# Two-stage kernel (log-space mixture, then attention over 32 images): the second stage's output taken in pieces of 1024 columns, and its fp32 products in two groups an image

## What is computed

```
x = x + L0(gn(x), accumulators)       # per position: log(exp(xs - max) @ exp(log_w - max)) + max + max
x = x + L1(gn(x), adj_w, affine_w, affine_b, ln_g, ln_b)

def L1(z):                            # z: 1024 x 128 for each image
    n = z / norm(z)                   # every row to length 1
    A = softmax(5 * (n @ adj_w @ n.T))            # 1024 x 1024
    h = A @ (z @ affine_w.T + affine_b)
    h = (h - mean(h)) / sqrt(var(h) + 1e-5) * ln_g + ln_b    # over the 128 channels
    return where(h >= 0, h, 0.01 * h)
```

## Time and profile before

| | |
|---|---|
| median of 3 runs | 1130.65 us (1130.39 to 1132.24) |
| the profiled execution | 1132.57 us, span 1130.8 us |
| busy share of the span | TensorE 93%, weight loads 70%, ScalarE 81%, VectorE 73%, GpSimd 49% |
| mean granted clock of TensorE | 0.988 |
| the chain that ended last | TensorE 85%, VectorE 7%, DMA 5% |
| HBM read, written | 136.45 MB, 20.31 MB |

### The profile page before, as it was taken

The page is one execution under the profiler, slowest core; times in us unless marked ns, Lnnn a source line. Parts: engine busy times, 40 slices in busy tenths (PEclk is TensorE's granted clock), DMA queues, the critical chain, the costliest instruction groups (busy, mean ns, idle before and its releaser), DMA issues.

```text
span 1130.8 us, 20986 instructions
## 1 busy us (share of the span) xinstructions
PE 1048.1 (93%) x7392; PEld 792.4 (70%) x7392; DVE 829.1 (73%) x1577; ACT 915.3 (81%) x1806; POOL 554.1 (49%) x391
## 2 busy tenths in 40 slices
PE   0189999959999999999999999999999999999995
PEld 0155555547777777777777777777777777777773
DVE  7822555588777777777777788787777777777776
ACT  0499999537888888888888888888888888888885
POOL 0044455503455555555555555555555555555543
PEclk9999999969999999999999999999999999999998
DMA  8979999830122222224322222222222222222213
GB/s 356 391 307 377 416 409 396 336 131 20 66 76 82 79 76 76 76 77 144 131 82 76 76 76 77 79 90 81 87 78 79 82 76 75 76 83 78 75 57 95
DMA packets 46903, 158.15 MB, mean 140 GB/s; under 512 B 5848, under 2 KB 6732, under 8 KB 36556
## 3 DMA queue, kind: packets, MB, share of 16 engines
q1 hardware_dynamic: 46796, 156.78, 37.2%
HBM read 136.45 MB, written 20.31 MB: 139 GB/s over the span
## 4 chain that ended last, share of the span: by engine, by line
PE 85%; DVE 7%; DMA 5%; ACT 1%; issue 1%; POOL 1%; SPq 0%; POOLq 0%; DVEq 0%; ACTq 0%
PE PS L1143 23%; PE PS L1144 21%; PE PS L1145 21%; DMA Wt<-acc 5%; PE PS L1161 5%; PE PS L1120 4%; DVE st L688 4%; PE PS L1110 3%; PE PS L1155 3%; PE PS L1131 2%; PE PS L1149 2%; DVE Pl L856 0%; PE PS L1178 0%; POOL hl L397 0%; ACT ET L457 0%
## 5 line engine op out<-in xcount | busy, mean ns | idle before, releaser
L856 DVE TENSOR_TENSOR Pl<-PS,Ph 128x512 fp32r<-128x512 f32 x512 | 347.5, 689 | 109.9 <-ACT PS L533 104.6
L533 ACT ACTIVATE PS<-PS 128x512 f32<-128x512 f32 x512 | 302.4, 601 | 0.5 <-PE PS L1145 0.5
L532 ACT ACTIVATE Ph<-PS 128x512 fp32r<-128x512 f32 x384 | 229.3, 597 | 55.1 <-PE PS L1145 54.8
L1143 PE MATMUL PS<-Ph,hh 128*128 128x512 f32 x512 | 210.4, 411 | 0.8 <-DVE Pl L856 0.8
L1143 PE MATMUL PS<-uTh,nTh 128*128 128x512 f32 x512 | 200.7, 392 | 0.0
L1144 PE MATMUL PS<-Pl,hh 128*128 128x512 f32 x512 | 200.4, 391 | 0.0
L412 POOL TENSOR_TENSOR X<-X 128x512 f32<-128x512 f32 x62 | 79.4, 1281 | 246.5 <-DVE X L878 246.5
L1145 PE MATMUL PS<-Ph,hl 128*128 128x512 f32 x512 | 200.0, 391 | 0.0
L1144 PE MATMUL PS<-uTl,nTh 128*128 128x512 f32 x512 | 199.9, 391 | 0.0
L1145 PE MATMUL PS<-uTh,nTl 128*128 128x512 f32 x512 | 199.9, 390 | 0.0
L378 POOL TENSOR_TENSOR LL<-LL 128x512 f32<-128x512 f32 x64 | 82.6, 1291 | 141.8 <-ACT LL L465 141.8
(11 more groups left out here) (126 smaller groups left out, 1708.6 us busy)
## 6 DMA issues: line engine op xcount, KB each, us to landing
Wt<-acc SPq DMA_DIRECT2D x64, 1024.0 KB, 7.5
X<-x SPq DMA_DIRECT2D x16, 1024.0 KB, 19.7
out<-X SPq DMA_DIRECT2D x64, 256.0 KB, 2.0
X<-factor_rows SPq DMA_DIRECT2D x63, 256.0 KB, 3.0
NU<-factor_rows SPq DMA_DIRECT2D x63, 256.0 KB, 3.5
SQ<-norm_rows SPq DMA_DIRECT2D x31, 512.0 KB, 3.6
out<-X SPq DMA_DIRECT2D x6, 512.0 KB, 4.7
X<-out SPq DMA_DIRECT2D x6, 512.0 KB, 6.4
```

The lines of the kernel that those rows point to most:

```text
L532: act.activation(Ph[:, g % RING, :], sl, ACT.Exp, scale=SHARP)
L533: act.activation(sl, sl, ACT.Exp, scale=SHARP).then_inc(weights_ready, 1)
L856: dve.tensor_tensor(Pl[:, r, :], SL[r], Ph[:, r, :].bitcast(F32), ALU.subtract)\
L1143: pe.matmul(out_, lh, rh, start=start, stop=False)
```

## The change

The output of an image is taken as one piece of 1024 columns from the moments on, where it was taken in two of 512:

- `values(b+1)` makes both halves in one go at k=4, into W0 and W1; `values_full`, `values_upper` (k=7) and `values_lower` are one instruction of 1024 columns each.
- `moments(b-1)` is one group behind the norms at k=7, four products of 2 x 256 columns. `deviation_roots` and `inverse_deviations` (k=10) are 256 wide.
- `scale_output`, `affine` (k=4), `leaky` (k=6) and `add_residual` are 1024 wide. Two pairs of 2 x 1024 take the place of three of 2 x 512, so seven images are sent away (AWAY = 7) and come back one an image.
- Moved: `inverse_norms` from k=9 to k=8, `tokens` from k=7 to k=11, `tokens_upper` from k=4 to k=1, `token_squares` from k=10 to k=14; on SyncE both puts stand before both loads; GpSimd's order is new.
- Image 0 keeps its values in halves, the last image (B-1) its output, under the names `first_...` and by `width`.

The diff, cut to its core (semaphore counts of unchanged steps and the last image's chain are left out):

```diff
-PAIR_ROOM = (5, 1, 2)
-PAIRS = len(PAIR_ROOM)
-
-AWAY = 6
+PAIR_ROOM = (1, 5)
+
+AWAY = 7
 BACK = 10
 CAST = (3, 7, 11, 14)
...
                     if b >= 2:
-                        store(b - 2, 0)
-                        if b - 2 < B - 1:
-                            store(b - 2, 1)
-                    if b == BACK:
-                        sp.wait_ge(stored, 16 * 2 * (BACK - 1))
-                        for i in range(AWAY):
-                            sp.wait_ge(spilled[i], 16)
-                            bring_back(i)
+                        store(b - 2)
+                    if 1 <= b + 2 < B:
+                        put_rn(b + 2)
                     if 1 <= b < B:
-                        load_rq(b - 1, 0)
-                        load_rq(b - 1, 1)
-                    if b == B - 1:
-                        load_rq(b, 0)
+                        put_rq(b - 1)
                     if 1 <= b + 2 < B:
                         load_rn(b + 2)
+                    if 1 <= b < B:
+                        load_rq(b - 1)
+                    if BACK <= b < BACK + AWAY:
+                        sp.wait_ge(stored, 16 * (BACK - 1))
+                        sp.wait_ge(spilled[b - BACK], 16)
+                        bring_back(b - BACK)
+                    if b == B - 1:
+                        put_rq(b)
+                        load_rq(b)
...
+            def values_lower(b):
+                pool.wait_ge(hh_ready, 2 * (b + 1))
+                s = HT * hslot(b, 0)
+                lower(hl_tiles[:, s:s + TT, :], room[3], hh_tiles[:, s:s + TT, :]).then_inc(hl_ready, 2)
...
             def attention():
                 for e in (0, 1):
-                    values_lower(0, e)
-                for b in range(B + 2):
-                    if 2 <= b <= B:
-                        add_residual(b - 2, 1)
+                    first_values_lower(e)
+                unit_tokens(1)
+                for b in range(B):
                     if b + 1 < B:
-                        unit_tokens(b + 1)
-                        if b:
-                            values_lower(b + 1, 0)
                         tokens_lower(b + 1)
-                        if b == 0:
-                            values_lower(b + 1, 0)
-                        values_lower(b + 1, 1)
-                    if 1 <= b <= B:
-                        scale_output(b - 1, 0)
-                    if 1 <= b < B:
-
-                        add_residual(b - 1, 0)
-                        scale_output(b - 1, 1)
+                    if b >= 2:
+                        add_residual(b - 2)
+                    if b + 1 < B:
+                        values_lower(b + 1)
+                    if b + 2 < B:
+                        unit_tokens(b + 2)
+                    if b:
+                        scale_output(b - 1)
+                scale_output(B - 1)
+                add_residual(B - 2)
...
-                        if k == (1 if b else 6) and b + 1 < B:
-                            values_upper(b + 1, 0)
-                        if k == 3:
-                            if 1 <= b <= B:
-                                take_output(b - 1, 1)
-                                deviation_roots(b - 1, 0)
-                        if k == (4 if b else 9) and b + 1 < B:
-                            values_upper(b + 1, 1)
-                        if k == 4 and b + 1 < B:
+                        if k == (1 if b else 4) and b + 1 < B:
                             tokens_upper(b + 1)
+                        if k == 3 and b:
+                            take_output(b - 1, 1)
+                        if k == 4 and b >= 2:
+                            affine(b - 2)
+                        if k == 7 and b + 1 < B:
+                            values_upper(b + 1)
                         if k == 8 and b + 2 < B:
                             norm_roots(b + 2)
-                        if k == 8 and 1 <= b <= B:
-                            deviation_roots(b - 1, 1)
+                        if k == (8 if b < B - 1 else 6) and b:
+                            deviation_roots(b - 1)
                         if k == 9 and b + 1 < B:
                             queries_upper(b + 1, 0)
-                        if k == 10 and b + 3 < B:
+                        if k == (14 if b else 10) and b + 3 < B:
                             token_squares(b + 3)
                         if k == 12 and b + 1 < B:
                             queries_upper(b + 1, 1)
-                        if k == (12 if b < B - 1 else 11) and b < B:
...
-            def inverse_deviations(b, e):
-                n = 2 * b + e
-                y = qms[e][:, 1, :]
-                w = (W0, W1)[e]
-                v = w[:, QH:2 * QH]
-                dve.wait_ge(q_roots, 2 * n + 2)
+            def inverse_deviations(b):
+                w = width(b) // Q
+                m = moments_of(b)
+                y, v = rows_of(b)[:, 1, :], m[:, w:2 * w]
+                dve.wait_ge(q_roots, 2 * b + 2)
                 dve.scalar_tensor_tensor(out=v, in0=v, scalar=-0.5, in1=y, op0=ALU.mult,
                                          op1=ALU.mult).then_inc(q_steps, 1)
-                dve.wait_ge(q_steps, 4 * n + 1)
+                dve.wait_ge(q_steps, 4 * b + 1)
                 dve.tensor_tensor(v, v, y, ALU.mult).then_inc(q_steps, 1)
-                dve.wait_ge(q_steps, 4 * n + 2)
+                dve.wait_ge(q_steps, 4 * b + 2)
                 dve.scalar_tensor_tensor(out=y, in0=v, scalar=1.5, in1=y, op0=ALU.add,
                                          op1=ALU.mult).then_inc(q_steps, 1)
-                dve.wait_ge(q_steps, 4 * n + 3)
-                dve.tensor_tensor(qms[e][:, 0, :], w[:, 0:QH], y, ALU.mult).then_inc(q_steps, 1)
-
...
-                        if k == (0 if b else 5) and b + 1 < B:
-                            values_full(b + 1, 0)
-                        if k == 0 and b >= 2:
-                            leaky(b - 2, 1)
-                        if k == (3 if b else 8) and b + 1 < B:
-                            values_full(b + 1, 1)
-                        if k == 4 and 1 <= b <= B:
-                            inverse_deviations(b - 1, 0)
+                        if k == 6 and b >= 2:
+                            leaky(b - 2)
+                        if k == (4 if b else 5) and b + 1 < B:
+                            values_full(b + 1)
                         if k == 7 and b + 2 < B:
                             clamp(b + 2)
+                        if k == 11 and b + 2 < B:
                             tokens(b + 2)
-                        if k == 8 and 1 <= b <= B:
-                            inverse_deviations(b - 1, 1)
                         if k == 9 and b + 1 < B:
                             queries_lower(b + 1, 0)
-                        if k == 9 and b + 2 < B:
+                        if k == 8 and b + 2 < B:
                             inverse_norms(b + 2)
+                        if k == (10 if b < B - 1 else 7) and b:
+                            inverse_deviations(b - 1)
                         if k == 12 and b + 1 < B:
...
-            def moments_into(w, pair):
+            def moments_into(w, pair, n):
                 for q in range(Q):
-                    last = pe.matmul(w[32 * q:32 * q + 32, 0:2 * QH], Dm[:, :], pair[:, :, q * QH:(q + 1) * QH],
+                    last = pe.matmul(w[32 * q:32 * q + 32, 0:2 * n], Dm[:, :], pair[:, :, q * n:(q + 1) * n],
                                      start=True, stop=True)
                 return last
...
+            def values(b):
+                pe.wait_ge(z_ready, b + 1)
+                pe.wait_ge(uTl_ready, 2 * b)
+                if b >= 3:
+                    pe.wait_ge(q_steps, 4 * (b - 2))
+                elif b == 2:
+
+                    pe.wait_ge(stat_steps, 4 * NS + 8)
+                else:
+                    pe.wait_ge(hf_ready, 2)
+                for e in (0, 1):
+                    values_into((W0, W1)[e], ZT[b % 2], e).then_inc(values_made, 1)
...
+            def moments(b):
+                if b == B - 1:
+                    pe.wait_ge(output_taken, 4 * b + 2)
+                    pe.wait_ge(uTl_ready, 2 * B)
+                else:
+                    pe.wait_ge(output_taken, 4 * (b + 1))
+                    if b + 2 < B:
+                        pe.wait_ge(hf_ready, 2 * (b + 3))
+                    else:
+                        pe.wait_ge(q_steps, 4 * b)
+                moments_into(moments_of(b), pairs[b % 2], width(b) // Q).then_inc(q_made, 1)
...
-                        if k == (0 if b else 5) and b + 1 < B:
-                            values(b + 1, 0)
-                        if k == (3 if b else 8) and b + 1 < B:
-                            values(b + 1, 1)
-                        if k == 3 and 1 <= b <= B:
-                            moments(b - 1, 0)
+                        if k == (4 if b else 5) and b + 1 < B:
+                            values(b + 1)
```

(24 more changed lines are left out.)

254 lines of the change are left out of this document (128 added, 126 removed).

## The result

The changed kernel takes 1178.36 us (median of 6 runs, 1176.54 to 1183.98) beside 1130.97 us of the kernel before (6 runs, 1127.78 to 1132.82): ratio 1.043, 95% interval 1.041 to 1.045. It is 4.3% slower, where 0.4% faster was forecast. The profiled execution has a span of 1175.7 us against 1130.8 before, 44.9 us more.

The account below looks back on a forecast made before the run. TensorE's issue bounds the kernel, 27.10 us an image. Groups -11.7, waits +4.4, ends +2.7 sum to -4.6: 1132.57 becomes 1128.0, and, as that execution is 1.9 above the median, 1126.0 us, range 1119.5 to 1140.

Parts of the forecast that it names:

- The fp32 groups: TensorE's three fp32 groups an image become two (k=4, k=7), saving 0.39 us an image, 11.7 us in all.
- The ring: Loop from one image's factor-row put through its output steps to the next put: 26.5 us against a 26.7 period.
- put and kept: Ring term: from the end of inverse_deviations(b-1), writing out the factor rows until kept, 1.76 us.
- GpSimd twice: Ring term: two GpSimd operations of 2.39 us each after the loads, 4.8 us.
- residual, values_lower and held step: Ring term: add_residual and values_lower on GpSimd, then inverse_norms on VectorE held by values_lower, 5.0 us.
- the rest: Ring term: what remains to the end of inverse_deviations(b), 4.4 us.
- The loads: Ring term: two factor-row loads on SyncE, 4.0 us today plus 1.2 for twice the bytes, 5.2 us.
- The tight place, k=6 to k=11: Chain from logits(6) to split 11: ready 14.71 us, wanted 14.69; TensorE waits 0.15 us an image, +4.4 us.
- The lock: At k=8, inverse_norms on VectorE is held until GpSimd's values_lower ends, finishing 0.28 us after it.
- Ends: Last image's longer output chain costs 2.5 us (bounds 0.5 to 3.5), the opening 0.2: +2.7 us.
- The first: Rival: TensorE never waits, the tight chain being shorter or VectorE not held: 1121.7 us; chance 0.25.
- The third: Rival: the ring becomes longer than the image because loads run long; at 6.2 us, 1145.7 us; chance 0.27.

Follow-up runs that it names:

- short_norm_load: Changed kernel, but from the third image on the norm row's load brings 64 columns (32 KB) instead of 1024: 1135.38 us, ratio 1.004.
- loads_first: Changed kernel with the norm row's load behind both factor-row loads, scale_output ahead of unit_tokens, tokens_upper at k=5: 1175.11 us, ratio 1.038.
- reorder: Changed kernel, inverse_deviations (k=8) ahead of inverse_norms (k=10), factor rows put and loaded before norm row, scale_output before unit_tokens, tokens_upper at k=5, deviation_roots before norm_roots: 1136.37 us.
- half_loads: Changed kernel, but from image 1 on each factor-row load brings 512 of 1024 columns (256 KB instead of 512 KB): 1131.25 us, ratio 1.001.
- reorder_clamp: reorder with the clamp on VectorE ahead of the split of unit 7 instead of behind it: 1122.49 us, ratio 0.992.
- reorder_tok: reorder with tokens_upper at k=4 and affine at k=5, so that tokens_lower is done before leaky: 1123.38 us, ratio 0.992.
- both_short: Changed kernel with factor-row loads of half the bytes (half_loads) and values_lower on 64 of 1024 columns: 1121.62 us, ratio 0.992.

## Why the prediction was wrong, point by point

**The fp32 groups: right.** Values: 856.05-854.04-0.227 = 1.78, forecast 1.78. Norms with moments: 861.78-860.01-0.227 = 1.54, forecast 1.54. Period without waits 26.70, forecast 26.7.

**The ring: the right mechanism with one term mis-sized, and too small a chance.** Its terms in the order of the prediction, forecast against the means over 16 images: put and kept 1.76 (the two starts it cites, 676.65 and 678.31 in the earlier trace rows, are 1.66 apart; the 0.10 more has no row) and 1.77; GpSimd twice 4.8 and 4.89; affine, weights, split and leaky 5.3 and 3.86+1.22 = 5.08; residual, values_lower and held step 5.0 and about 5.1 (L856 ends 2.7 after values_lower starts); the rest 4.4 and about 4.5. All lie within 0.25. The loads: 5.2 forecast, 7.41 measured, and this is the step that failed. It took 1.2 us out of bounds of 0.1 and 3.5 for twice the bytes, nearer to the row of one load by itself, landing after 3.6. What it left out stands in the prediction's own sentence, that three transfers of 512 KB start within 1.5 us of each other: the norm load was given no price in the sum. It alone costs the factor loads 1.6 to 2.0 us (short_norm_load, loads_first). Factor loads with nothing ahead take 5.3 to 5.4 (loads_first and the reorder kernels), where 5.2 was forecast. The mean DMA share of 0.25, set against the rival, says nothing of the 4 us in which the three transfers overlap and the share is 0.92 to 1.00.

The consequence was worked out rightly: by the prediction's rule, each microsecond of loads beyond 5.4 lengthens each image by as much, and 7.41 gives images of 28.7 and 30 x 1.6 + 2.7 = 51 us more, beside 45 measured. But the margin of 0.2 us between a ring of 26.5 and a period of 26.7 was given 0.27 with a term in it whose bounds lay 3.4 us apart. The middle of these bounds, 5.8, is already where the kernel gets slower.

**The tight place, k=6 to k=11: right in place, close in price, and not the only one.** Where the loads' ring is open and the order is the changed kernel's, images take 26.92 to 26.97 (half_loads), 0.25 above the floor; forecast 0.15. The wait stands at attend of unit 11, behind the held L856, the inverse deviations, the cast and split 11, as forecast. The prediction followed splits to attend, but not the clamp and queries_lower to the queries. In the changed kernel these two end TensorE's longest waits, and the clamp gives reorder its only one.

**The lock: right.** Forecast: L856 starts inside values_lower and ends 0.28 after it. Measured: values_lower 865.25 to 867.66, L856 865.41 to 867.93, in the window from 300 to 1100 us in all 28 images, mean 2.48 instead of 0.42. The section "SBUF: two separate sides" of the page "SBUF — State Buffer" in the Trainium skill says that such a VectorE operation, with two inputs in SBUF, and a GpSimd operation that reads SBUF exclude each other for the whole instruction of whichever starts first. The trace now agrees for operations of 2.4 us as well; a split, with one input in PSUM, keeps its 0.69 beside them. What wasn't foreseen is the same lock on leaky, as soon as tokens_lower is moved (1.94 instead of 1.22).

**Ends.** From the first logits of the last image to the end of the span 40.6 us before, 43.8 after and 43.4 in reorder_clamp: +2.8 to +3.2, forecast 2.5. The first logits come some 3 us earlier than before (245.4 against 248.7), which the prediction had as 0.2 later; why stays open.

**The rivals.** The first, no wait (1121.7), describes reorder_tok, reorder_clamp and both_short to within 2 us, kernels that don't have the ring's problem. The third came true, with a time beyond its own figure of 1145.7 and beyond the range, which took in only two thirds of it.

## What to carry to other kernels

Where a change doubles transfers and puts three of them in a row, price the last one together with all that are issued just ahead, also those for another purpose. The mean share of the DMA engines doesn't show such a crowd; their share in the few us around the transfers does. A loop-carried chain that fits the period with 0.2 us to spare, and has a term known only to 3 us, should be weighed as the likely outcome. When a cure moves other work, sum the ring again with the moved work in it: loads_first gained 2.0 us in one term and lost 1.9 in two others.

## What the runs showed of the hardware

A load of 512 KB from one row to 128 partitions lands after 3.6 us by itself; of two in a row the second lands after 4.9, counted from its own issue, and with a third issued 1.1 us ahead of them the three land after 3.9, 5.5 and 6.8. With the three under way the DMA engines were 92% and 100% busy, at 303 and 293 GB/s (846 to 848 and 848 to 850 us of the changed kernel). A put of the factor rows takes 1.77 us to be kept, and 2.51 with such a load under way. Leaky, 1024 columns on VectorE, took 1.93 instead of 1.22 where it started (699.16) inside tokens_lower on GpSimd (697.62 to 700.01) and went on after it.
